# Attention scores and row maxima as pairs of 64-row array tiles, with the PSUM banks redistributed

## The reference

```python
Xn = (X - mu) * rsqrt(var + EPS) * ln_g + ln_b
Q, K, V = split_heads(Xn @ Wq + bq), split_heads(Xn @ Wk + bk), split_heads(Xn @ Wv + bv)
scores = einsum('bhqd,bhkd->bhqk', Q, K) / sqrt(16)
A = softmax(where(causal, scores, -inf), axis=-1)
x = layernorm(X + einsum('bhqk,bhkd->bhqd', A, V) @ Wo + bo)      # heads merged before Wo
h = relu(x @ W1 + b1)
alpha = softmax(h @ W2 + b2)                                      # 8 weights per row
out = layernorm(x + sum_k alpha_k * (U_k @ (V_k @ x)))            # rank 64 for each k
```

## Time and profile before

| what | value |
|---|---|
| median of 3 runs | 511.62 us (510.28 to 512.27) |
| span of the profiled execution | 510.6 us |
| PE busy | 454.6 us, 89% |
| DVE busy | 324.8 us, 64% |
| ACT busy | 218.8 us, 43% |
| mean granted PE clock | 0.961 of full speed |

### The profile page before, as it was taken

The page is one execution under the profiler, slowest core; times in us unless marked ns, Lnnn a source line. Parts: engine busy times, 40 slices in busy tenths (PEclk is TensorE's granted clock), DMA queues, the critical chain, the costliest instruction groups (busy, mean ns, idle before and its releaser), DMA issues.

```text
span 510.6 us, 6947 instructions
## 1 busy us (share of the span) xinstructions
PE 454.6 (89%) x2512; PEld 265.5 (52%) x2512; DVE 324.8 (64%) x780; ACT 218.8 (43%) x470; POOL 71.0 (14%) x97
## 2 busy tenths in 40 slices
PE   0289799999999999999899995999999999999693
PEld 0145565556546554357557752555655554447352
DVE  6936588678778674526476894478868855114276
ACT  1132034666666756333421131466666757532110
POOL 9720010022011010100400010012102001010000
PEclk9999699999999999799999997699999999999897
DMA  5006990025002000000423195006100000000011
GB/s 165 0 10 108 213 161 7 3 46 83 3 0 85 2 2 1 0 1 3 117 66 62 36 168 89 1 3 112 15 1 2 3 2 1 0 1 1 0 42 42
DMA packets 13266, 21.18 MB, mean 41 GB/s; under 512 B 2352, under 2 KB 9776, under 8 KB 13232
## 3 DMA queue, kind: packets, MB, share of 16 engines
q1 hardware_dynamic: 13232, 20.73, 19.5%
HBM read 5.78 MB, written 2.10 MB: 15 GB/s over the span
## 4 chain that ended last, share of the span: by engine, by line
PE 77%; DVE 12%; ACT 4%; DMA 2%; issue 2%; SPq 2%; DVEq 0%; ACTq 0%
PE ps L691 24%; PE ps L758 18%; PE ps L778 15%; PE ps L736 13%; PE ps L740 3%; DVE mx L582 3%; DVE nv L521 2%; PE ps L685 2%; ACT pr L483 2%; SPq L388 1%; PE ps L788 1%; DVE st L533 1%; DMA stq<-mrow 1%; DVE x L540 1%; PE ps L823 1%
## 5 line engine op out<-in xcount | busy, mean ns | idle before, releaser
L483 ACT ACTIVATE pr<-ps 128x512 f32<-128x512 f32 (+3 forms) x384 | 171.7, 493 | 164.4 <-PE ps L758 162.6
L582 DVE TENSOR_REDUCE mx<-ps 128x1 f32<-128x512 f32 (+3 forms) x304 | 185.3, 655 | 58.9 <-PE ps L740 40.7
L758 PE MATMUL ps<-stq,stk 98*128 98x512 f32 (+3 forms) x384 | 146.0, 414 | 11.8 <-DMA stq<-mrow 6.7
L736 PE MATMUL ps<-stk,stq 96*128 96x512 f32 (+3 forms) x384 | 136.0, 391 | 3.6 <-DMA stq<-qk 1.4
L758 PEld LDWEIGHTS ps<-stq,stk 98*128 98x128 f32 x384 | 71.5, 197 | 83.2 <-ACT pr L483 44.5
L448 POOL TENSOR_SCALAR_AFFINE_SELECT pr<-pr 128x512 f32<-128x512 f32 x64 | 40.9, 639 | 359.1 <-ACT pr L483 359.1
L736 PEld LDWEIGHTS ps<-stk,stq 96*128 96x128 f32 x384 | 76.0, 200 | 14.5 <-DVE mx L582 5.5
L778 PE MATMUL ps<-pr,va 128*32 128x512 f32 (+3 forms) x768 | 83.5, 507 | 0.0
L740 PE MATMUL ps<-mask,ident_b 128*128 128x128 bf16 x256 | 58.8, 237 | 0.0
L740 PEld LDWEIGHTS ps<-mask,ident_b 128*128 128x128 bf16 x256 | 25.6, 100 | 30.9 <-issue 23.1
L691 PE MATMUL ps<-pr,w_qk 128*128 128x512 f32 x64 | 31.8, 646 | 3.8 <-ACT pr L462 3.8
(11 more groups left out here) (72 smaller groups left out, 340.1 us busy)
## 6 DMA issues: line engine op xcount, KB each, us to landing
stk<-qk SPq DMA_DIRECT2D x16, 256.0 KB, 3.8
stq<-qk SPq DMA_DIRECT2D x32, 128.0 KB, 3.8
x_in<-in_x SPq DMA_DIRECT2D x8, 256.0 KB, 3.5
stk<-qk SPq DMA_DIRECT2D x16, 128.0 KB, 3.7
stq<-qk SPq DMA_DIRECT2D x32, 64.0 KB, 3.1
out_y<-x SPq DMA_DIRECT2D x3, 512.0 KB, 2.9
qk<-in_x SPq DMA_DIRECT2D x2, 512.0 KB, 4.0
v_t<-in_vt SPq DMA_DIRECT2D x1, 512.0 KB, 5.8
```

The costliest lines, as they stand in the source:

```text
L483: nc.scalar.activation(probs(b, g, s)[:, j, q0 - c * CHUNK:], act_bank(ev)[:, q0 - c * CHUNK:], ACT.Exp, scale=DH ** -0.5).then_inc(s_act_ ...
L582: nc.vector.tensor_reduce(dst, src, AX.X, ALU.max).then_inc(s_dve_free, 1)
L736: last = nc.tensor.matmul(bank[:, i * w:(i + 1) * w], q[0:ROWS, t // TPC, j, tile(t % TPC)], k[0:ROWS, k0 // CHUNK, j % 2, 0:w], start=Tru ...
L758: nc.tensor.matmul(bank[:, q0 - c * CHUNK:], stk[stack_of(b, g)][0:ROWS + 2, kt // TPC, j % 2, tile(kt % TPC)], stq[stack_of(b, g)][0:ROWS ...
```

## The change

- `ROWS` becomes 48: each head has its own half of the array's rows. Heads 0 and 1 of a pair stand at partitions 0 and 64 (`strip(i)`), with their own copy of keys and queries and their own maxima rows. There are no zero rows. Slot `m` picks one of two such pairs, so `score` and `max` events take two heads.
- A score event issues two matmuls (one for each 64-row half) into two adjacent banks, and ACT takes both in one exponential of 128 x 1024. There are 2 such events in a step instead of 4.
- A max unit covers both halves with `n` slots each: n = 2 up to 256 keys, else 1. It writes two banks, and DVE empties each with a reduce of its own (the event is listed twice, with i = 0 and 1; PE acts at the first and waits there for both banks). There are 20 units for each group, 160 in all, 12 of the 20 on the diagonal. The mask is one matmul for each bank over all its slots, behind all score matmuls of the unit.
- `DVE_RING` is 3 and `ACT_RING` 4. The banks of the ACT ring are given out by a table, pairs at even places.
- A stack event has eight DMAs (four for `stk`, four of the same shapes as before for `stq`), a rows event two.
- `course` is 9 units before the first score, 24 at step 4, all 80 at step 37, and the rows follow 2 units behind a split instead of 3.
- POOL fills `stk` with -1 instead of `stq` with 0.

```diff
-DVE_RING, ACT_RING = 4, 3
+DVE_RING, ACT_RING = 3, 4
-ROWS = 2 * 3 * DH
+ROWS = 3 * DH
+HALF = P // 2
...
-            n = 4 if w == P else 2 if w == 2 * P else 1
-            units += [(t, k0, w, tuple(range(j, j + n)), k0 + w == (t + 1) * P) for j in range(0, HPG, n)]
+            n = 2 if w <= 2 * P else 1
+            units += [(t, k0, w, m, n, k0 + w == (t + 1) * P) for m in range(0, 2, n)]
...
-    course = [(0, needed[0] + 6), (first_step[1], needed[1] + 8), (first_step[-1] - 3, needed[-1])]
+    course = [(0, needed[0] + 3), (first_step[1], needed[1] + 4), (first_step[-1] - 3, needed[-1])]
...
-                due.append((issued + 3, g, c))
+                due.append((issued + 2, g, c))
...
-        for j in range(HPG):
+        for m in range(2):
...
-    return order
+    return [part for ev in order for part in ([(*ev, i) for i in range(2)] if ev[0] == "max" else [ev])]
...
+        act_at, act_before = {}, {}
+        filled, at = [0] * ACT_RING, 0
+        for ev in n_act:
+            two = ev[0] == "score"
+            at = (at + (at % 2 if two else 0)) % ACT_RING
+            act_at[ev] = DVE_RING + at
+            act_before[ev] = max(filled[at:at + 1 + two])
+            filled[at:at + 1 + two] = [n_act[ev]] * (1 + two)
+            at = (at + 1 + two) % ACT_RING
...
+        def strip(i, n=ROWS):
+            return slice(i * HALF, i * HALF + n)
...
-                    loads = [(k[two, c], qk[heads, 1, :, c]), (k[one, c], qk[heads, 1, 0, c])]
+                    loads = []
                     for i in range(2):
                         head = slice((2 * g + i) * DH, (2 * g + i + 1) * DH)
+                        both, one = strip(i, 2 * DH), slice(i * HALF + 2 * DH, i * HALF + ROWS)
                         high = qk[head, 0, 0, c].rearrange("p m s -> p (m s)").unsqueeze(1)
-                        loads += [(q[2 * i * DH:2 * (i + 1) * DH, c, 2 * i:2 * i + 2], high.to_broadcast([DH, 2, KC * CHUNK])),
-                                  (q[one.start + i * DH:one.start + (i + 1) * DH, c, 2 * i:2 * i + 2], qk[head, 0, 1, c])]
+                        loads += [(k[both, c], qk[head, 1, :, c]), (k[one, c], qk[head, 1, 0, c]),
+                                  (q[both, c], high.to_broadcast([DH, 2, KC * CHUNK])), (q[one, c], qk[head, 0, 1, c])]
...
-                    sp.dma_start(stq[stack_of(b, g)][ROWS:ROWS + 2, c].bitcast(F32),
-                                 mrow[:, c, :].bitcast(F32)).then_inc(s_rows[c], 16)
+                    for i in range(2):
+                        sp.dma_start(stq[stack_of(b, g)][i * HALF + ROWS:i * HALF + ROWS + 2, c].bitcast(F32),
+                                     mrow[i * 4 * TPC:(i + 1) * 4 * TPC, c, :].bitcast(F32)).then_inc(s_rows[c], 16)
...
-                    nc.scalar.activation(probs(b, g, s)[:, j, q0 - c * CHUNK:], act_bank(ev)[:, q0 - c * CHUNK:],
+                    nc.scalar.activation(probs(b, g, s).rearrange("p (i m) q -> p i m q", i=2)[:, :, m, q0 - c * CHUNK:],
+                                         act_pair(ev)[:, :, q0 - c * CHUNK:],
                                          ACT.Exp, scale=DH ** -0.5).then_inc(s_act_free, 1)
...
-                    bank = take_dve(ev)
-                    for i, j in enumerate(heads):
-                        last = nc.tensor.matmul(bank[:, i * w:(i + 1) * w], q[0:ROWS, t // TPC, j, tile(t % TPC)],
-                                                k[0:ROWS, k0 // CHUNK, j % 2, 0:w], start=True, stop=not diagonal)
-                        if diagonal:
-
-                            last = nc.tensor.matmul(bank[:, (i + 1) * w - P:(i + 1) * w], ident_b[:], mask[:],
-                                                    start=False, stop=True)
-                    last.then_inc(s_dve_full, 1)
+                    take_dve(("max", b, g, u, 1))
+                    banks = [dve_bank(("max", b, g, u, i)) for i in range(2)]
+                    for m in range(n):
+                        for i in range(2):
+                            last = nc.tensor.matmul(banks[i][:, m * w:(m + 1) * w], q[strip(i), t // TPC, m0 + m, tile(t % TPC)],
+                                                    k[strip(i), k0 // CHUNK, m0 + m, 0:w], start=(m == 0),
+                                                    stop=(m == n - 1 and not diagonal))
+                            if m == n - 1 and not diagonal:
+                                last.then_inc(s_dve_full, 1)
+                    if diagonal:
+
+                        for i in range(2):
+                            nc.tensor.matmul(banks[i][:, 0:n * w].rearrange("p (m k) -> p m k", k=w)[:, :, w - P:],
+                                             ident_b[:], mask[:].unsqueeze(1).to_broadcast([P, n, P]),
+                                             start=False, stop=True).then_inc(s_dve_full, 1)
...
-                    bank = take_act(ev)
-                    nc.tensor.matmul(bank[:, q0 - c * CHUNK:], stk[stack_of(b, g)][0:ROWS + 2, kt // TPC, j % 2, tile(kt % TPC)],
-                                     stq[stack_of(b, g)][0:ROWS + 2, c, j, q0 - c * CHUNK:],
-                                     start=True, stop=True).then_inc(s_act_full, 1)
+                    take_act(ev)
+                    for i in range(2):
+                        last = nc.tensor.matmul(act_pair(ev)[:, i, q0 - c * CHUNK:],
+                                                stk[stack_of(b, g)][strip(i, ROWS + 2), kt // TPC, m, tile(kt % TPC)],
+                                                stq[stack_of(b, g)][strip(i, ROWS + 2), c, m, q0 - c * CHUNK:],
+                                                start=True, stop=True)
+                    last.then_inc(s_act_full, 1)
```

More of the change, by code:

```diff
@@ L88, in attention_order @@
     for k in range(len(at) + 3):
-        for j in range(HPG):
+        for m in range(2):
             if k < len(at):
-                if j == 0 and k in first_step:
+                if m == 0 and k in first_step:
                     n = first_step.index(k)
@@ L95, in attention_order @@
                         order.append(("rows", b, *due.pop(0)[1:]))
-                order.append(("score", b, *at[k], j))
-            issue_max(int(target(k + (j + 1) / HPG)))
+                order.append(("score", b, *at[k], m))
+            issue_max(int(target(k + (m + 1) / 2)))
             for behind, when, kind in ((2, 0, "drain"), (3, 1, "turn")):
-                if j == when and 0 <= k - behind < len(at) and steps[at[k - behind][1]][3]:
+                if m == when and 0 <= k - behind < len(at) and steps[at[k - behind][1]][3]:
                     order.append((kind, b, at[k - behind][0], steps[at[k - behind][1]][0]))
             more = beside.get(k, [])
-            order += more[j * len(more) // HPG:(j + 1) * len(more) // HPG]
+            order += more[m * len(more) // 2:(m + 1) * len(more) // 2]
         if 0 < k <= len(at):
@@ L196, in block_kernel @@
     G = HEADS // HPG
-    PAIRS = HPG // 2
     units, steps = max_units(T), score_steps(T)
@@ L229, in block_kernel @@
         va = sb("va", [P, T, HEADS, VW])
-        stq = [sb(f"stq{i}", [P, C, HPG, CHUNK], F32R) for i in range(STACKS)]
-        stk = [sb(f"stk{i}", [P, C, PAIRS, CHUNK], F32R) for i in range(STACKS)]
+        stq = [sb(f"stq{i}", [P, C, 2, CHUNK], F32R) for i in range(STACKS)]
+        stk = [sb(f"stk{i}", [P, C, 2, CHUNK], F32R) for i in range(STACKS)]
         pr = [sb(f"pr{i}", [P, HPG, CHUNK]) for i in range(PROBS)]
-        mx = sb("mx", [P, 2, C, C, HPG, TPC])
-        mhl = sb("mhl", [P, 2, 2, HPG, TPC], F32R)
+        mx = sb("mx", [P, 2, C, C, 2, 2, TPC])
+        mhl = sb("mhl", [P, 2, 2, 2, 2, TPC], F32R)
         mrow = sb("mrow", [2 * HPG * TPC, 2, P], F32R)
@@ L409, in _ @@
             pool.memset(ident[:], 0.0).then_inc(s_ident, 1)
-            pool.memset(stq[0][0:ROWS].bitcast(F32), 0.0).then_inc(s_stack_init, 1)
+            pool.memset(stk[0][:].bitcast(F32), -1.0).then_inc(s_stack_init, 1)
             pool.wait_ge(s_ident, 1)
@@ L423, in _ @@
             for i in range(1, STACKS):
[L424 to L429, removed]
+                pool.memset(stk[i][:].bitcast(F32), -1.0).then_inc(s_stack_init, 1)
             for ev in order:
@@ L444, in _ @@
                     blk = probs(b, g, s)[:, :, q0 % CHUNK:q0 % CHUNK + P]
-                    pool.wait_ge(s_act_free, n_act["score", b, g, s, HPG - 1])
+                    pool.wait_ge(s_act_free, n_act["score", b, g, s, 1])
                     pool.affine_select(out=blk, in_=blk, compare_op=ALU.is_ge, fill=0.0, base=0,
@@ L573, in _ @@
                 if kind == "max":
-                    _, _, g, u = ev
-                    t, k0, w, heads, _ = units[u]
+                    _, _, g, u, i = ev
+                    t, k0, w, m, n, _ = units[u]
                     dve.wait_ge(s_dve_full, n_dve[ev])
-                    if t % TPC == 0 and k0 == 0 and heads[0] == 0 and b * G + g >= 2:
```

(19 more changed lines are left out.)

29 lines of the change are left out of this document (14 added, 15 removed).

## The result

The changed kernel takes 541 us where the kernel before takes 511: the ratio is 1.059, 95% interval 1.055 to 1.064. The prediction said 532 us, slower.

What follows compares the result with a forecast made beforehand. PE was taken to bound steady attention and SP the start of a batch's attention; 510.6 + 9.9 (steady steps) + 9.0 (SP) + 1.5 (the rest) = 531.0, plus 1.0 to the median, 532 us; range 518 to 545.

Steps and rivals of the forecast that it cites:

- PE bound before, SP at the starts: Kernel before: PE sets the pace in steady attention, 2.80 us a step; SP's issues set it where a batch's attention starts.
- PE's work after: Steady steps: fewer score and maxima slots, less added mask and switch time, sum -0.56, so PE needs 2.24 us of 2.80.
- The rival of a serial pair: Score and maxima pairs: halves do not run beside each other, each pair pays a second weight load; 560 us, chance 0.12.
- The mask term: Diagonal max units: switching from 64-row tiles to the full array for masks adds 0.54 us a step, 0.12 without a drain.
- Pairs in three banks: Max units in steady steps: PE waits for two of three banks until DVE's first reduce; full-width diagonal cycle 1.50 us.
- My 2.95 us a step: Steady steps 4 to 37: 2.95 us each, between 2.80 and 3.1, giving +9.9 us over 66 steps.
- SP +9.0: Starts of both batches: SP's extra stack and rows issues add 9.0 us, from +4 to +11.
- +6.3 us in full at step 4 of batch 1: Batch 1, step 4: SP is the last link, so four longer stacks and a second rows issue cost 4 x 1.4 + 0.7.
- The other SP terms: Batch 0: first stacks and first rows +2.0 us; at step 4, +0.7 us for the second rows issue.
- POOL's memsets at nothing: POOL's changed memsets: slack, so no effect on the time.
- The value groups: Sign in batch 0's attention: value groups 2.95 us apart if right, less than 2.64 us apart if wrong.

Runs made afterwards that it cites:

- full-row kernel: The changed kernel with every score and maxima matmul over all 128 rows, stq zeroed by POOL first, so no row tiling; 547 us, ratio 1.071.

## Why the prediction was right, and where it was not

- **PE bound before, SP at the starts.** Held. Cutting DVE's work left the kernel before unchanged, and the order of SP's issues alone moved it by 8 us.
- **PE's work after.** The halves run beside each other, as reckoned: row tiling takes the steady part from 116.3 us to the 105.0 reckoned for full clock, -11.3 us a batch. The rival of a serial pair was wrong. The mask term was too large. The sum had 0.33 + 0.10 + 0.24 + 0.10 = 0.77 us for a diagonal unit, so 0.54 for its masks; the rows after show 0.32 + 0.21 = 0.53 us from the pair to the next one, so about 0.30.
- **Pairs in three banks.** The mechanism is there (58.4 us of weight loads held up by DVE, before 5.5), and with the order that came with it it costs 12.0 us a batch, seen without row tiling. I forecast +9.9 us in two batches for this and PE's saving together. Near full clock they cancel: a step took 2.75 us in the six steps, before 2.72. The forecast put it 0.15 us above before.
- **The step that failed: the clock.** My 2.95 us a step let every steady step run at clock 1.00, as in the earlier trace rows. They ran at 0.79 in batch 0 and 0.80 in batch 1, and took 3.4 us. By the price above this is 17 us in batch 0 and 16 in batch 1 of the profile, all of its steady loss of 33.5 us. There is no profile of the executions at 541 us; they had some 24 us less of half clock and were 9 us shorter, so the loss there is smaller by about that. No rival named the clock.
- **SP +9.0.** The same issues cost the kernel before +16 us, lower clock included. In the changed kernel the largest term, +6.3 us in full at step 4 of batch 1, did not come: PE waited 1.08 us there instead of 6.06, and steps 0 to 4 took 24.4 us instead of 26.1, at a clock of 0.50 (before 0.77). The other SP terms I can't separate, since these parts hold them together with other things; moving the loads showed no gain there.
- **POOL's memsets at nothing.** Wrong, and to the change's favour: PE's first matmul starts at 13.1 us instead of 21.5 (last section). It hid up to 8.4 us of the loss, of which 3.4 are left at step 0 (69.4 us, before 72.8).

That the sum came near is in part luck. In the profile the steady steps lost 33.5 us where the sum had 9.9, because the clock was left out, and all the rest lost 4.4 where the sum had 10.5; the total was 37.9 against 20.4. The executions at 541 us lost 30. The value groups had exposed it: 2.95 us a step was to be right, and they lie 3.4 us apart on average, (171.4 - 90.2) / 24. What stays open: why, with the same instructions, the clock falls in some executions and steps and not in others; whether fewer rows at work or PE's pauses, which row tiling lengthens, take it down in the changed kernel; and what the switches at the masks alone would give back. None was tried by itself.

## What to carry to other kernels

Before halving the work of a TensorE-bound stage, ask what else then runs short: whether the engine, with more pauses and over fewer rows, still keeps its granted clock, and whether a unit that takes two banks of three leaves its reader anything to work on. Read the clock of each window first, and compare stretches at equal clock; a total hides it. Where many DMA issues stand ahead of one that the next stage needs, both their number and their order count: in the kernel before, two more in each stack and one in each rows event cost 16 us, and moving twelve behind the one that was needed gave 8.

## What the runs showed of the hardware

**A PE that is always busy can be granted half clock.** Row-tiled matmuls over 50 of 128 rows, one after the other, ran at 0.50 (1.2 of 2.4 GHz) with PE busy for 59.92 of 60 us, and full rows at 1.00 with PE busy for 106.06 of 116.3 us. The Trainium skill, TensorE: Matmul & The Clock Gate, What's actually happening, has the gate follow how busy PE has been; the first of these windows disagrees, unless busy means more than that a matmul is running. What else decides is not shown: no run varied the rows alone at equal work and equal waits.

**A small operation of DVE waits through several of POOL's memsets.** Timelines of DVE and of POOL at the start, before:

```profile
6.35 8.08 DVE L521 TENSOR_SCALAR nv<-mv 128x4 f32<-128x4 f32 x1
14.47 1.83 DVE L522 TENSOR_SCALAR nv<-nv 128x4 int32<-128x4 int32 x1
```

```profile
7.45 6.96 POOL L424 MEMSET stq<- 96x4096 f32 x2
14.47 5.51 POOL L428 MEMSET stk<- 2x2048 f32 x3
```

and after:

```profile
6.23 3.09 DVE L532 TENSOR_SCALAR nv<-mv 128x4 f32<-128x4 f32 x1
9.35 0.17 DVE L533 TENSOR_SCALAR nv<-nv 128x4 int32<-128x4 int32 x1
```

```profile
5.74 3.55 POOL L439 MEMSET stk<- 128x2048 f32 x2
```

A 128 x 4 operation takes 8.08 us, until the two stq memsets end at 14.41, and the next one 1.83 us, the length of one of the three stk memsets (5.51 / 3); after the change it takes 3.09 us, until 9.29, and its successor 0.17. The full-row kernel, with both kinds of memset, has 8.28 us again. The Trainium skill, SBUF — State Buffer, SBUF: two separate sides, says that DVE and GpSimd hold a shared port pair for a whole instruction. The trace agrees, and DVE here did not get it between the two stq memsets either, but it did between those and the stk memsets. The wait lies on the path of both kernels' first microseconds.
